# Last batch of layer 2: its first two contraction tiles as three products of halves, with their raw edges loaded one step earlier

## The reference

```
x = x + x @ W.T + 0.5 * (x @ A0[label]) @ B0.T          # layer 0
x = x + dequant(quant(x))                               # layer 1
x = x + x @ weight[adapter].T                           # layer 2
x = x + (x @ B3[adapter].T) @ A3[adapter].T             # layer 3
```

## Time and profile before

| | us |
|---|---|
| median of 3 runs | 459.86 |
| lowest and highest | 459.11, 460.87 |
| the profiled execution, its own time | 459.77 |
| its span, first to last instruction | 458.0 |
| PE busy in the span | 446.3 (97%) |
| DVE busy | 423.1 (92%) |
| ACT busy | 357.5 (78%) |
| POOL busy | 34.6 (8%) |

### The profile page before, as it was taken

The page is one execution under the profiler, slowest core; times in us unless marked ns, Lnnn a source line. Parts: engine busy times, 40 slices in busy tenths (PEclk is TensorE's granted clock), DMA queues, the critical chain, the costliest instruction groups (busy, mean ns, idle before and its releaser), DMA issues.

```text
span 458.0 us, 7875 instructions
## 1 busy us (share of the span) xinstructions
PE 446.3 (97%) x3118; PEld 408.1 (89%) x3118; DVE 423.1 (92%) x409; ACT 357.5 (78%) x330; POOL 34.6 (8%) x46
## 2 busy tenths in 40 slices
PE   7999999999999999999999999999999998999995
PEld 6899999889898999989998999989998998998784
DVE  4889999999899998999899998999969999999983
ACT  5699999987799777977799775997569958676730
POOL 1000011010101000000101000110100101000000
PEclk9999999999999999999999999999999999999999
DMA  7963453596359835687459835486353626378022
GB/s 287 334 241 105 92 135 100 134 224 212 82 167 244 248 89 151 184 220 228 82 180 232 244 92 149 143 215 174 76 188 117 168 63 166 122 212 318 1 92 92
DMA packets 35352, 75.62 MB, mean 165 GB/s; under 512 B 3956, under 2 KB 14068, under 8 KB 34548
## 3 DMA queue, kind: packets, MB, share of 16 engines
q1 hardware_dynamic: 30420, 61.50, 40.3%
q0 software_dynamic: 4896, 13.63, 16.8%
HBM read 53.10 MB, written 8.39 MB: 134 GB/s over the span
## 4 chain that ended last, share of the span: by engine, by line
PE 64%; DVE 23%; issue 8%; DMA 2%; ACT 2%; SPq 1%; DVEq 0%; ACTq 0%
PE l_ps L925 31%; PE l_ps L990 18%; DVE quant L784 8%; DVE cand L758 6%; PE l_ps L1002 5%; PE l_ps L1018 3%; DVE cand L766 2%; DVE x L736 2%; PE bx_ps L951 2%; PE bx_ps L1037 2%; DVE quant L778 1%; DMA a_raw<-a 1%; PE l_ps L935 1%; DVE x L835 1%; DMA adapter_ids<-adapters 1%
## 5 line engine op out<-in xcount | busy, mean ns | idle before, releaser
L990 PE MATMUL l_ps<-x,w_sb 128*128 128x256 f32 x672 | 150.3, 380 | 0.9 <-DVE x L736 0.9
L784 DVE COPY_PREDICATED quant<-mask,cand 128x2048 f32<-128x2048 int8 (+2 forms) x77 | 146.0, 1897 | 0.4
L990 PEld LDWEIGHTS l_ps<-x,w_sb 128*128 128x128 f32 x672 | 125.9, 190 | 19.4 <-issue 2.1
L566 ACT ACTIVATE cand<-x,inv_delta 128x2048 f32<-128x2048 f32 (+2 forms) x88 | 134.4, 1527 | 8.8 <-DVE quant L778 7.0
L576 ACT ACTIVATE mask<-magnitude,thr_bias 128x2048 fp8e5<-128x2048 f32 (+2 forms) x77 | 117.5, 1526 | 9.0 <-DVE quant L784 8.2
L758 DVE TENSOR_SCALAR cand<-cand,delta 128x2048 f32<-128x2048 f32 (+2 forms) x88 | 87.6, 996 | 7.7 <-ACT cand L566 7.4
L766 DVE TENSOR_SCALAR cand<-cand,lower,upper 128x2048 f32<-128x2048 f32 (+2 forms) x88 | 92.8, 1055 | 0.4
L925 PE MATMUL l_ps<-x_hi,w_hi 128*128 128x256 f32 x512 | 86.1, 290 | 1.9 <-ACT w_hi L467 1.0
L925 PE MATMUL l_ps<-x_hi,w_lo 128*128 128x256 f32 x512 | 82.8, 283 | 0.0
L925 PE MATMUL l_ps<-x_lo,w_hi 128*128 128x256 f32 x512 | 82.5, 283 | 0.0
L925 PEld LDWEIGHTS l_ps<-x_hi,w_hi 128*128 128x128 f32 x512 | 71.0, 191 | 7.7 <-issue 4.1
(11 more groups left out here) (84 smaller groups left out, 384.6 us busy)
## 6 DMA issues: line engine op xcount, KB each, us to landing
w_sb<-w SPq DMA_DIRECT2D x60, 384.0 KB, 3.8
out<-x SPq DMA_DIRECT2D x32, 256.0 KB, 2.3
x_raw<-x SPq DMA_DIRECT2D x15, 512.0 KB, 5.9
w_edge<-w SPq DMA_DIRECT2D x28, 256.0 KB, 3.5
w_lo<-w_edge POOLq DMA_DIRECT2D x28, 256.0 KB, 4.7
x_lo<-x_raw POOLq DMA_DIRECT2D x6, 1024.0 KB, 8.6
cand<-w SPq DMA_DIRECT2D x7, 512.0 KB, 7.6
x<-a SPq DMA_DIRECT2D x7, 512.0 KB, 3.4
```

The lines of the kernel that those rows point to most:

```text
L566: act.activation(cand[:, c % CANDS, 0:n], x2_unit(u), ACT.Identity, bias=ROUND, scale=inv_delta[:, k:k + 1]).then_inc(rounded, 1)
L784: dve.copy_predicated(y, mask[:, m % MASKS, 0:n].bitcast(I8), t).then_inc(merged, 1)
L990: last = nc.tensor.matmul(l2_bank(b, q)[:, i * S:(i + 1) * S], w2_block(b, o, k), x2[:, b % SLOTS, k * S:(k + 1) * S], start=(i == 0 and k ...
```

## The change

The last batch's contraction tiles 0 and 1 become products of halves, like those of the other batches. Part 0 on TensorE (`last_first_part`) is now first tiles 2 and 3 in float32 for all eight outputs, then, for all eight, three products for each of the tiles 0 and 1. Their halves go into what layer 0 has left free: those of the weights into slot 0 of `x_hi` and `x_lo` (last used by batch 6), those of x2 into the first 512 columns of slot 1 (used by batch 7).

```diff
+            def last_first_part():
+                b = B - 1
+                pe.wait_ge(x0_done, 2 * B)
+                pe.wait_ge(x2_done, LAST + 1)
+                for o in range(T):
+                    pe.wait_ge(last_w2_loaded[o], 16)
+                    for k in range(EDGE, PARTS[1]):
+                        nc.tensor.matmul(l2_bank(b, o // 2)[:, o % 2 * S:(o % 2 + 1) * S], w2_block(b, o, k),
...
+                pe.wait_ge(x2_split_done, B)
+                x2h, x2l = x2_halves(b)
+                for o in range(T):
+                    if o >= RING:
+                        pe.wait_ge(last_edge_added[o - RING], 16)
+                    elif o % 2 == 0:
+                        pe.wait_ge(w2_added[o // 2], 16 * B)
+                    hi, lo = last_edges(x_hi, o, 1), last_edges(x_lo, o, 1)
+                    for w, v in ((hi, x2h), (hi, x2l), (lo, x2h)):
+                        for k in range(EDGE):
...
-            last_layer2(0)
+            last_first_part()
```

ScalarE splits the edges in two pairs in unit 8 and one by one in unit 9, and makes the high part of x2; POOL adds the raw edges and subtracts for the low part of x2:

```diff
                 elif u == LAST:
+                    if j == 1:
+                        split_last_pair(0)
...
+                    if j == 4:
+                        split_last_pair(1)
                     if j == 5:
                         split_edges(s - 1, 3)
+                elif u == LAST + 1:
+                    if j in (1, 2, 3, 4):
+                        split_last_edge(RING + j - 1)
+                    if j == 1:
+                        split_last_x2()
...
+            def split_last_x2():
+                act.wait_ge(l0_done, 2 * B)
+                act.wait_ge(x2_done, LAST + 1)
+                act.activation(x2_halves(B - 1)[0], x2[:, (B - 1) % SLOTS, 0:EX], ACT.Copy).then_inc(x2_hi_done, 1)
...
+                if s == SPLIT:
+                    for q in range(2):
+                        add_last_pair(q)
                 add_edges(s - 1, 3)
...
+            add_last_edge(RING)
+            hi, lo = x2_halves(B - 1)
+            pool.wait_ge(x2_hi_done, B)
+            pool.tensor_tensor(lo, x2[:, (B - 1) % SLOTS, 0:EX], hi.bitcast(F32), ALU.subtract)\
+                .then_inc(x2_split_done, 1)
+            for o in range(RING + 1, T):
+                add_last_edge(o)
```

SyncE loads the edges of outputs 0 to 3 in step s = 6, behind `load_edges(6, 1)` and ahead of `load_w2(6, 1)`, with one more read of an adapter id, and no longer in step 7:

```diff
                     load_edges(s, 1, adapter)
+                    if s == B - 2:
+                        last_adapter = adapter_of(B - 1)
+                        for o in range(RING):
+                            load_last_edge(o, last_adapter)
                     load_w2(s, 1, adapter)
...
-                    for o in range(RING):
-                        load_last_edge(o, adapter)
```

More of the change, by code:

```diff
@@ L128, in build @@
         last_w2_loaded = [sem(f"last_w2_loaded{o}") for o in range(T)]
+        last_edge_loaded = [sem(f"last_edge_loaded{o}") for o in range(T)]
+        last_edge_added = [sem(f"last_edge_added{o}") for o in range(RING, T)]
         w2_used = sem("w2_used")
@@ L238, in split_pair, with last_edges, x2_halves @@
             return tiles[:, first:first + 2, :]
+        def last_edges(halves, first, n):
+            return halves[:, 0, first * EW:(first + n) * EW]
+        def x2_halves(b):
+            if b == B - 1:
+                return x_hi[:, b % 2, 0:EX], x_lo[:, b % 2, 0:EX]
+            return x2_hi[:, :], x2_lo[:, :]
         def a3_raw(b):
@@ L245, in b3_tile, with edge_count @@
             return m[:, k * w:(k + 1) * w]
+        def edge_count(b, q):
+            return 4 * b + q + (3 if (b, q) == (SPLIT - 1, 3) else 1)
         fold = parts[:, 0:QUAD]
@@ L343, in store @@
                     sp.wait_ge(out_done, b * 4 + q + 1)
-                elif q == 3:
-                    sp.wait_ge(last_out_done, 1)
+                elif q in ADDED_UP:
+                    sp.wait_ge(last_out_done, ADDED_UP.index(q) + 1)
                 else:
-                    sp.wait_ge(out_done, b * 4 + q + 1)
+                    sp.wait_ge(out_done, b * 4 + [p for p in LAST_ORDER if p not in ADDED_UP].index(q) + 1)
                 sp.dma_start(out[b, q], x3[:, q * CW:(q + 1) * CW]).then_inc(out_stored[q], 16)
@@ L676, in _ @@
             split_bx(B - 1)
-            act.wait_ge(l3_done, 4 * (B - 1) + LAST_ORDER.index(3) + 1)
-            act.activation(x3[:, 3 * CW:4 * CW], l3_bank(B - 1, 3), ACT.Copy).then_inc(last_out_done, 1)
+            for q in ADDED_UP:
+                act.wait_ge(l3_done, 4 * (B - 1) + LAST_ORDER.index(q) + 1)
+                act.activation(x3[:, q * CW:(q + 1) * CW], l3_bank(B - 1, q), ACT.Copy).then_inc(last_out_done, 1)
         @block.vector
@@ L896, in _ @@
             for q in LAST_ORDER:
-                if q != 3:
+                if q not in ADDED_UP:
                     finish(b, q)
@@ L1005, in layer2 @@
                     last.then_inc(l2_done, 1)
+            def last_first_part():
[6 more added lines that the diff above has]
+                        nc.tensor.matmul(l2_bank(b, o // 2)[:, o % 2 * S:(o % 2 + 1) * S], w2_block(b, o, k),
+                                         x2[:, b % SLOTS, k * S:(k + 1) * S], start=(o % 2 == 0 and k == EDGE),
+                                         stop=False)
+                pe.wait_ge(x2_split_done, B)
[8 more added lines that the diff above has]
+                        for k in range(EDGE):
+                            nc.tensor.matmul(l2_bank(b, o // 2)[:, o % 2 * S:(o % 2 + 1) * S],
+                                             w[:, k * P:(k + 1) * P], v[:, k * S:(k + 1) * S],
+                                             start=False, stop=False)
             def last_layer2(part, quarters=range(4)):
                 b = B - 1
-                if part == 0:
-                    pe.wait_ge(x0_done, 2 * B)
                 pe.wait_ge(x2_done, LAST + part + 1)
@@ L1014, in last_layer2 @@
                         o = 2 * q + i
-                        if part == 0:
-                            pe.wait_ge(last_w2_loaded[o], 2 * 16)
                         for k in range(PARTS[part], PARTS[part + 1]):
@@ L1020, in last_layer2 @@
                                                     x2[:, b % SLOTS, k * S:(k + 1) * S],
-                                                    start=(i == 0 and k == 0), stop=(i == 1 and k == T - 1))
+                                                    start=False, stop=(i == 1 and k == T - 1))
                     if part == len(PARTS) - 2:
@@ L1050, in layer3 @@
                     pe.wait_ge(a3_split_done, b + 1)
-                on_x3 = b == B - 1 and q == 3
+                on_x3 = q in ADDED_UP
                 for i in range(2):
@@ L1056, in layer3, with add_up @@
                 last.then_inc(l3_done, 1)
+            def add_up(q):
+                for i in range(2):
+                    nc.tensor.matmul(l3_bank(B - 1, q)[:, i * S:(i + 1) * S], ident[:, :],
+                                     x3[:, (2 * q + i) * S:(2 * q + i + 1) * S], start=(i == 0), stop=False)
             def layer3_pair(b, q):
@@ L1108, in _ @@
                 low_rank3(B - 1, q)
-            for i in range(2):
-                nc.tensor.matmul(l3_bank(B - 1, 3)[:, i * S:(i + 1) * S], ident[:, :],
-                                 x3[:, (T - 2 + i) * S:(T - 1 + i) * S], start=(i == 0), stop=False)
+            for q in ADDED_UP:
+                add_up(q)
             for q in LAST_ORDER:
```

33 lines of the change are left out of this document (28 added, 5 removed).

## The result

The changed kernel takes 464.06 us (median of 5 runs, 463.19 to 465.61), where the kernel before took 459.86. The ratio is 1.0095, with a 95% interval of 1.0079 to 1.0110: slower by about 4.2 us. The forecast was 460.4 us in a range of 459.1 to 461.9.

The account below looks back on a forecast made before the run. The chain through VectorE was taken to bound the end; TensorE's 1.1 us was absorbed, and ScalarE's 0.1 plus POOL's 0.4 us delayed it: 459.77 + 0.5 + 0.09 = 460.4 us, range 459.1 to 461.9.

Parts of the forecast that it names:

- TensorE's saving: Part 0 on TensorE: 16 products as halves, 0.363 us a tile pair instead of 0.431, 1.09 us less.
- The wait of the earlier trace for output 0: Ahead of part 0, waiting for output 0's weights: goes as SyncE's loads come earlier, 0.25 us less.
- the forecast wait for output 3: TensorE in part 0: new wait for output 3's weights, taken as 0.2 us, between 0 and 0.45.
- Absorbed at `sum_bx(6)`: TensorE arrives 1.1 us earlier but waits there for ScalarE's `parts`; idle time grows from 0.37 to about 1.5 us.
- Worth nothing at the end: TensorE's 1.1 us gain disappears in the wait at `sum_bx(6)`, so the kernel's end does not move earlier.
- ScalarE and SyncE: ScalarE's added edge and x2 work delays VectorE's chain 0.1 us (0 to 0.9); SyncE's four added loads are free.
- the price of POOL's subtraction: Delay to VectorE's chain from POOL's subtraction for x2's low part: taken as 0.4 us.
- The lower end: Lower bound on the subtraction's price: 0, as a merge beside a POOL DMA issue showed nothing of it.
- The upper end: Upper bound on the subtraction's price: 1.1 us, if VectorE stands still for the whole of it.
- place between VectorE's: Reason given for 0.4 us: POOL's subtraction fits between VectorE's instructions, partly beside one that reads PSUM.
- The rival in which POOL is kept waiting by VectorE: POOL's subtraction can't begin, so low part and edges come late for TensorE; at worst 473.6 us, chance 0.08.
- The rival of a full hold: VectorE stands still for all of POOL's subtraction: 1.1 us plus ScalarE's 0.1, 461.1 us, chance 0.27.

Follow-up runs that it names:

- e2: Changed kernel with x2's low part made by ScalarE's negative and an adding DMA from POOL, no POOL subtraction; 460.71 us.
- e1: Kernel before plus only POOL's 128x512 subtraction, its result unused; 461.04 us.
- f3: Changed kernel with POOL's adding DMA for output 4's edge issued behind its subtraction instead of ahead of it; 463.00 us.
- f4: Kernel before plus a POOL subtraction of 1536 columns, its result unused; 464.66 us.
- g2: Changed kernel, POOL's subtraction kept, with `sum_bx(6)` behind part 1's second quarter and part 0's float32 outputs ordered 4 to 7, 0 to 3; 461.04 us.
- e3: Changed kernel with 14 unused identity products on TensorE filling the idle time ahead of `sum_bx(6)`; 462.00 us.
- e4: Changed kernel with `sum_bx(6)` moved behind the second quarter of part 1 instead of the first; 461.20 us.
- f1: Changed kernel with e2's and e4's edits and part 0's float32 products in output order 4 to 7, 0 to 3; 458.59 us.
- g1: e2 with part 0's float32 products in output order 4 to 7, 0 to 3, `sum_bx(6)` not moved; 460.51 us.
- g3: g2 with x2's low part subtracted on VectorE instead of POOL; 459.45 us.
- f2: Kernel before with `sum_bx(6)` moved behind the second quarter of part 1; 459.13 us.

## Why the prediction was wrong

**TensorE's saving: right.** Part 0 runs from 418.02 to 431.31 us, 13.29 us with 0.27 us of waiting, so 13.02 where the earlier trace rows give 13.98: 0.96 us less, 1.09 forecast. The rows of halves follow each other at 0.12 us a record, which was the working's 0.121. From the anchor `low_rank3` starts 1.15 us earlier, where 1.1 was forecast. The wait of the earlier trace rows for output 0 went, and the forecast wait for output 3 came with 0.27 us, between 0 and 0.45.

**Absorbed at `sum_bx(6)`: right in direction.** The saving ended in that wait. "Worth nothing at the end" was wrong, see below.

**ScalarE and SyncE: right.** All of after's other work in unit 9 left 0.06 us beside the hold, 0.1 forecast. The four edge loads issued at 359.63 us in 2.04 us, and nothing that the trace shows waited for them:

```profile
359.63 2.04 SPq L321 DMA_DIRECT2D x_raw<-w  x4
361.85 1.18 SPq L305 DMA_DIRECT2D w_sb<-w  x2
```

**The first step that failed: the price of POOL's subtraction.** The sum took 0.4 us between 0 and 1.1. Measured was 1.78, outside the bounds. Two things were wrong. The lower end rested on the earlier trace rows, a merge beside a POOL DMA issue; but e2 shows that an issue alone costs a scaling 0.15 us, and e1 that arithmetic costs 0.82: the row was of another kind of instruction on both sides, and could not bound this one. I then took the value near it without a row that spoke for it. The upper end took the subtraction as 1.13 us at most, four times a 128-column row; it takes 1.27 to 1.59, and VectorE is released only 0.28 us after its end. The op found no "place between VectorE's": whichever scaling or clipping met it stood still. The rival in which POOL is kept waiting by VectorE did not come either: the subtraction began at 414.92 us, and no idle time stands ahead of the halves.

The Trainium skill, "SBUF — State Buffer", section "Who interferes with whom", says that the pair of ports that VectorE and GpSimd share is locked for a whole instruction. The traces agree: e1, f3 and f4 show a stop to the end of POOL's instruction, for 0.82, 1.03 and 3.00 us. In after, g2, e3 and e4 it was the instruction whose record begins first, by 0.37 to 0.38 us, that was stopped, and not the later one as the prediction had it; a DMA issue of POOL was running then.

The rival of a full hold, 461.1 us with a chance of 0.27, should have been the forecast: its hold of 1.1 us is near what a subtraction costs with nothing ahead of it (0.82 in e1, at 461.04 us, and 1.03 in f3), and the prediction itself called it the likelier. For the changed kernel it too was 0.7 us short on the hold and had nothing of the clock.

**The second step that failed: "the saving is worth nothing at the end".** I treated idle time as free. TensorE came 1.15 us earlier and `parts` 1.8 us later, and both went into one gap: 0.37 + 1.15 + 1.8 = 3.3 us, against 1.5 forecast. A gap of that size let the clock fall, and cost 1.49 us on its far side. e3, which fills the gap with useless work, has the clock at 1.00 and is back by 1.5 us. That TensorE's gain itself did harm is argued, not isolated. The nearest pair is e1 and f3, with holds of 0.82 and 1.03 us: e1, without the saving, was idle for 1.28 us, takes 461.04 us and had no low clock in 10 executions; f3, with it, was idle for 3.14 us, takes 463.00 us and had 4 in 6. f3 also has the change's other work. No rival had this mechanism, and so the range ended at 461.9.

**Around the span.** Kernels in which the split reads and adds the last edges (after, and e2 to e4, f1, g1 to g3) have a median of 1.95 to 2.2 us around the span, f3 2.6; those without (before, e1, f2, f4) 1.77 to 1.82. Some 0.3 us of the 4.2 is this. I had carried 1.77 us over unchanged. What it is stays open.

**The sum, corrected,** for the profiled execution: 459.77 + 0.24 (start) + 1.78 (hold) + 0.06 + 1.49 (clock) + 0.49 (around the span) = 463.83, measured 463.86. It is an account of this trace, and closes because its terms are read from it; the hold and the clock's price have runs of their own (e1, e2 and f4; e3).

**Where the room was.** In the profile of before part 2 starts 1.62 us after unit 10 is done. I read that as TensorE running on after the wait, and did not ask whether the wait could stand elsewhere. f2 is 0.8 us faster by moving one call.

## What to carry to other kernels

Arithmetic moved to GpSimd beside a VectorE that works back to back is not free: here 512 columns held it for 0.82 to 1.03 us, and for 1.78 us behind a DMA issue. Forecast it as a hold to the end of GpSimd's instruction, look at what stands directly ahead on its queue, and compare it with the time that VectorE would need itself (0.6 us in g3). When one engine is made earlier and the engine it waits for later, add both to the gap between them, and compare the gap with those at which your own traces and runs show TensorE's granted clock low; then move the wait later or fill it. Look at the step that ties two engines together before making either faster.
